# A graph layer pair: the first pair's X and W2 loaded in halves, its hop 2 taken by chunks

## The chip, the cores and the metric
The kernel runs on one core of one Trainium2 chip. The metric is the device time of one execution in microseconds. A profiled execution gives, beside its time, a span: from the first to the last instruction that the profiler recorded.

## The reference
64 graphs of 128 nodes with 256 features, an adjacency `adj` per graph. Two layers, each followed by a residual sum and a layer norm:

```python
def _L0_gnn_ref(X, A, Wv, bv, aw, ab, Wk, bk):
    Xw = X @ Wv + bv
    sj = Xw @ aw[:d, 0]
    si = Xw @ aw[d:, 0]
    e = leaky_relu(sj[:, None, :] + si[:, :, None] + ab[0], 0.2)
    alpha_matrix = A * exp(e)
    transition = alpha_matrix / (sum(alpha_matrix, -1, keepdims=True) + 1e-12)
    H = 0; Xk = X
    for k in range(3):
        H = H + Xk @ Wk[k] + bk[k]
        Xk = einsum('bij,bjd->bid', transition, Xk)
    return relu(H)
def _L1_gnn_ref(x, adj, w):
    return einsum('bnf,fo->bno', einsum('bnm,bmf->bnf', adj, x), w)
x = _layernorm(x + _L0_gnn_ref(x, adj, ...))
x = _layernorm(x + _L1_gnn_ref(x, adj, L1_gnn_w))
```

## The kernel before
The 64 graphs are worked on as 32 pairs. X comes transposed (`xt`), 128 features per partition row and two chunks `c` of the contraction over 256 features; in SBUF a pair's X is laid out chunk, graph, node, so the first 256 columns are chunk 0 of both graphs. W2 (`Wk[2]`) lies in `WY_sb` with the two chunks of its rows beside each other.

The hops are reordered: a pair's products are X W2 ("hop 2", to `ps_y`), then the transition times that plus X W1 ("hop 1", `ps_v`), then the transition times that plus X W0 ("hop 0", `ps_h`). From the second pair on each f32 product is three float32r products, of high and low parts that ScalarE (high), VectorE and GpSimd (low) split off. The first pair cannot wait for the split: `first_hop2`, `first_hop1` multiply the f32 tiles themselves; each such product shows as two matmul records.

The scores need `u`, which `score_weights` (L1177) makes from WvT and the `vectors` (aw and bv), two columns per chunk, into `ps_out`. VectorE copies u beside W1 and W2 (L575, L576), splits W2 with its u columns (L579, L581), then W0's low part (L583), and then makes the `shift` of the scores (L588). ScalarE's `first_scores` (L401) waits for hop 1 and for the shift. TensorE transposes the scores (`spread_scores`, L1084), from which ScalarE makes leaky, exp and the high part of alpha, and so on.

Each engine has its program in an order written out by hand. Five queues matter. SyncE issues the loads of X, WvT, W1; waits until X is there; then W0, X of pair 1, and so on. ScalarE issues W2, the vectors, bk, ab, and then its first activation, `XT_hi` of pair 0 (behind a load of the activation table). TensorE's order at the start is nine products of ones (`keep_warm`, 512 columns each, results unused), `first_hop2(0)` (graph 0, both chunks), `score_weights`, `first_hop2(1)`, `first_hop1(0)`, `score_shift`, `first_hop1(1)`, `sum_of_biases`, `spread_scores(0)`, `hop0(0)`, hop 2 of pair 1. VectorE's is given above. GpSimd makes bv_aw from the vectors and then the low parts of X (L901). After the opening, a loop of steps over the pairs follows, one pair per step, with products of several pairs interleaved.

Of the kernel before, what the change touches and what calls it, by code (L numbers as in the profile page):

```python
# [10 lines left out]
P = 128  # L11
PER = 2
DMA = 16
# [5 lines left out]
def resnorm_graph_kernel(nc, xt, adjs, nodes, WvT, vectors, ab, Wk, bk, w, si_rows, out):  # L19
    PAIRS = nodes.shape[0]  # L20
    D = w.shape[0]
    C = D // P
# [3 lines left out]
    with ExitStack() as ctx:  # L26
        def sb(name, shape, dt=F32):
            return ctx.enter_context(nc.sbuf_tensor(name, shape, dt))

        def ps(name, shape):  # L30
            return ctx.enter_context(nc.psum_tensor(name, shape, F32))

        def sem(name):
            return ctx.enter_context(nc.semaphore(name))


        xt_sb = [sb(f"xt{s}", [P, C * PER * P]) for s in range(4)]
# [7 lines left out]
        WY_sb = sb("WY_sb", [P, C, D + 2])  # L45
# [66 lines left out]
        ps_v = ps("ps_v", [P, PER, 512])  # L112
        ps_y = ps("ps_y", [P, PER, 512])
# [10 lines left out]
        xt_loaded = [sem(f"xt_loaded{s}") for s in range(4)]  # L124
        adjs_loaded = [sem(f"adjs_loaded{s}") for s in range(5)]
        nodes_loaded = [sem(f"nodes_loaded{s}") for s in range(2)]
        stored = [sem(f"stored{s}") for s in range(3)]
        WvT_loaded = sem("WvT_loaded")
        vectors_loaded = sem("vectors_loaded")
        ab_loaded = sem("ab_loaded")  # L130
        bk_loaded = sem("bk_loaded")
        Wk_loaded = [sem(f"Wk{n}_loaded") for n in range(HOPS)]
# [107 lines left out]
        def loads(k, slots=2):  # L240
            return DMA * (k // slots + 1)
# [41 lines left out]
        def _(sp):  # L283
            def load_xt(k):
                if k == 4:

                    sp.wait_ge(v1_done, 1)
                if k >= 4:
                    sp.wait_ge(xt_lo_ready, k - 3)
                sp.dma_start(xt_sb[k % 4][:], xt[k]).then_inc(xt_loaded[k % 4], DMA)  # L290
# [37 lines left out]
                sp.dma_start(to[:, :, 0:D], Wk[n].rearrange("(c p) n -> p c n", p=P)).then_inc(Wk_loaded[n], DMA)  # L328


            load_xt(0)
            sp.dma_start(WvT_sb[:], WvT.rearrange("(c p) n -> p c n", p=P)).then_inc(WvT_loaded, DMA)
            load_Wk(1)
            sp.wait_ge(xt_loaded[0], DMA)
# [39 lines left out]

        @block.scalar
        def _(act):
            act.dma_start(WY_sb[:, :, 0:D], Wk[2].rearrange("(c p) n -> p c n", p=P)).then_inc(Wk_loaded[2], DMA)
            act.dma_start(vectors_sb[:].rearrange("p c n -> p (c n)"), vectors).then_inc(vectors_loaded, DMA)
            act.dma_start(bk_sb[:], bk).then_inc(bk_loaded, DMA)
            act.dma_start(ab_col[:], ab.partition_broadcast(P)).then_inc(ab_loaded, DMA)  # L380

            def xt_hi(k):

                act.wait_ge(xt_loaded[k % 4], loads(k, 4))
                act.activation(XT_hi[k % 7][:].rearrange("p c b i -> p (c b i)"),  # L385
                               xt_sb[k % 4][:], ACT.Copy).then_inc(xt_hi_ready, 1)
# [108 lines left out]
            def step(k):  # L495
# [23 lines left out]
                if there(k + 6):  # L519
                    xt_hi(k + 6)  # L520
# [11 lines left out]
                if k == LAST - 1:  # L532
                    late_sum_of(LAST - 3)

            xt_hi(0)
            wx_hi(0)
            v2_hi(0)
            xt_hi(1)
            first_scores()
            xt_hi(2)  # L540
# [30 lines left out]
        def _(dve):  # L571
# [3 lines left out]
            dve.tensor_copy(W1_sb[:, :, D:D + 2], ps_u).then_inc(u_ready, 1)  # L575
            dve.tensor_copy(WY_sb[:, :, D:D + 2], ps_u).then_inc(u_ready, 1)  # L576
            dve.wait_ge(u_ready, 2)
            dve.wait_ge(Wk_loaded[2], DMA)
            dve.tensor_copy(WY_hi[:], WY_sb[:]).then_inc(WY_hi_ready, 1)  # L579
            dve.wait_ge(WY_hi_ready, 1)  # L580
# [419 lines left out]
        def _(pe):  # L1000
# [25 lines left out]
            def first_product(to, weights, b):  # L1026

                X = xt_sb[0][:].rearrange("p (c b i) -> p c b i", c=C, b=PER)
                for c in range(C):
                    last = pe.matmul(to, X[:, c, b], weights[:, c], start=c == 0, stop=c == C - 1,  # L1030
                                     skip_group_check=True)
                return last

            def first_hop2(b):
                pe.wait_ge(xt_loaded[0], DMA)
                pe.wait_ge(Wk_loaded[2], DMA)
                last = first_product(ps_y[:, b, 0:D], WY_sb[:, :, 0:D], b)
                if b == PER - 1:
                    last.then_inc(y_done, 1)

            def first_hop1(b):

                pe.wait_ge(Wk_loaded[1], DMA)
                pe.wait_ge(u_ready, 1)
                last = first_product(ps_v[:, b, 0:D + 2], W1_sb, b)
                if b == PER - 1:
                    last.then_inc(v1_done, 1)
# [99 lines left out]
            def keep_warm(to, times):  # L1147

                for n in range(times):
                    pe.matmul(to, some[:, 0:P], some, start=True, stop=True, skip_group_check=True)  # L1150
# [26 lines left out]
            def score_weights():  # L1177

                pe.wait_ge(vectors_loaded, DMA)
                pe.wait_ge(WvT_loaded, DMA)  # L1180
                for c in range(C):
                    for j in range(C):
                        last = pe.matmul(ps_u[:, c], WvT_sb[:, j, c * P:(c + 1) * P], vectors_sb[:, j, 0:2],
                                         start=j == 0, stop=j == C - 1, skip_group_check=True)
                last.then_inc(u_done, 1)
# [38 lines left out]
                    aggregate(k - 1)  # L1224
                hop2_and_scores(k + 5, [1] if k == 1 else range(PER))

            keep_warm(ps_v[:, 0], 9)
            first_hop2(0)
            score_weights()
            first_hop2(1)  # L1230
            first_hop1(0)
            score_shift()
            first_hop1(1)
# [64 lines left out]
```

## Time and profile before

| | us |
|---|---|
| median of 3 runs (277.46 to 281.25) | 277.48 |
| profiled execution, its time | 277.04 |
| profiled execution, its span | 275.2 |
| TensorE busy | 268.7 (98%) |
| VectorE busy | 210.8 (77%) |
| GpSimd busy | 196.8 (72%) |
| ScalarE busy | 188.8 (69%) |

Busy times are sums over instructions in the profiled execution; an engine busy for 98% of the span still may hold short waits. PE is TensorE, PEld its weight load, DVE VectorE, ACT ScalarE, POOL GpSimd, SP SyncE; SPq and ACTq are their queues, which issue DMAs. The median is 0.44 us above the profiled execution's time.

### The profile page before, as it was taken

Reading aid. Unit: us, or ns where it says so; the run is one execution under the profiler, and the core shown is the slowest. Engines: PE = TensorE matmul, PEld = TensorE weight load, DVE = VectorE, ACT = ScalarE, POOL = GpSimd, SP = SyncE. Lnnn points to the kernel's source line nnn. Section 1 sums busy time; section 2 is a strip of 40 time slices with the busy share of each in tenths; the row PEclk is TensorE's granted clock in tenths of the full one; section 3 lists DMA queues with packets and bytes.
Section 4 is the critical chain, followed back from the end, with each engine's and each line's share of the span. In section 5 each row is a group of like instructions: output and inputs, shape, how many; then the busy total and the mean of one; then the engine's idle time right before and its main releaser. Section 6 shows DMA issues by size and latency. Waiting matters only on the chain.

```text
span 275.2 us, 6489 instructions
## 1 busy us (share of the span) xinstructions
PE 268.7 (98%) x2199; PEld 263.0 (96%) x2199; DVE 210.8 (77%) x562; ACT 188.8 (69%) x428; POOL 196.8 (72%) x420
## 2 busy tenths in 40 slices
PE   8999999999999999999999999999999999999992
PEld 4899999999999999999999999999999999999991
DVE  0787887877778787777878777787877777788874
ACT  2788866677766677776667777666777765666643
POOL 3565577778877777887777788777777777557574
PEclk9999999999999999999999999999999999999998
DMA  7955367957845585348585278556773394912304
GB/s 228 301 138 79 117 101 172 116 132 111 148 128 157 154 144 70 126 138 153 141 154 151 81 110 137 147 148 155 133 97 51 108 124 105 126 50 80 114 0 152
DMA packets 28614, 34.92 MB, mean 127 GB/s; under 512 B 7075, under 2 KB 16422, under 8 KB 28582
## 3 DMA queue, kind: packets, MB, share of 16 engines
q1 hardware_dynamic: 27872, 33.99, 58.1%
q10 hardware_dynamic: 710, 0.53, 0.6%
q8 instruction: 17, 0.28, 0.4%
q14 instruction: 15, 0.12, 0.1%
HBM read 26.09 MB, written 8.42 MB: 125 GB/s over the span
## 4 chain that ended last, share of the span: by engine, by line
PE 91%; DVE 3%; POOL 2%; DMA 1%; issue 1%; ACT 0%; DVEq 0%; POOLq 0%
PE ps_h L1004 24%; PE ps_v L1004 17%; PE ps_y L1004 15%; PE ps_out L1004 14%; PE ps_agg L1160 10%; PE ps_v L1100 3%; PE ps_v L1104 3%; PE ps_v L1102 3%; DMA WY_sb<-Wk_dram 1%; PE ps_agg L1004 1%; PE ps_y L1030 1%; PE ps_v L1030 1%; POOL rstd L877 1%; POOL res L888 0%; DVE WX_lo L817 0%
## 5 line engine op out<-in xcount | busy, mean ns | idle before, releaser
L642 DVE SCALAR_TENSOR_TENSOR ps_h<-ps_h,inv_rowsum,bias 128x256 f32<-128x256 f32 x60 | 26.5, 488 | 22.7 <-PE ps_h L1004 22.7
L901 POOL TENSOR_TENSOR XT_lo<-xt,XT_hi 128x512 fp32r<-128x512 f32 x32 | 41.5, 1300 | 3.0 <-ACT XT_hi L385 1.4
L913 POOL TENSOR_TENSOR alpha<-exps,adjs 128x256 f32<-128x256 f32 x31 | 22.9, 738 | 23.3 <-ACT exps L428 23.3
L1004 PE MATMUL ps_v<-WX_hi,XT_hi 128*128 128x256 f32 x128 | 36.7, 287 | 0.3 <-DVE ps_v L648 0.2
L1004 PE MATMUL ps_v<-WX_lo,XT_hi 128*128 128x256 f32 x128 | 36.0, 282 | 0.0
L1004 PE MATMUL ps_v<-WX_hi,XT_lo 128*128 128x256 f32 x128 | 36.0, 281 | 0.0
L1004 PE MATMUL ps_h<-WX_hi,XT_hi 128*128 128x256 f32 x124 | 35.0, 282 | 0.0
L1004 PE MATMUL ps_h<-WX_lo,XT_hi 128*128 128x256 f32 x124 | 35.0, 282 | 0.0
L1004 PE MATMUL ps_h<-WX_hi,XT_lo 128*128 128x256 f32 x124 | 34.9, 282 | 0.0
L459 ACT ACTIVATE y<-res,offset,rstd 128x256 f32<-128x256 f32 x62 | 33.6, 591 | 1.6 <-POOL offset L868 1.5
L917 POOL TENSOR_TENSOR alpha_lo<-alpha,alpha_hi 128x256 fp32r<-128x256 f32 x31 | 22.7, 733 | 15.9 <-ACT alpha_hi L437 15.9
L1004 PE MATMUL ps_y<-WY_hi,XT_hi 128*128 128x258 f32 x112 | 34.1, 304 | 0.0
L1160 PE MATMUL ps_agg<-adjs,y 128*128 128x128 f32 x248 | 32.7, 274 | 0.0
L1004 PE MATMUL ps_y<-WY_lo,XT_hi 128*128 128x258 f32 x112 | 31.7, 283 | 0.0
L1004 PE MATMUL ps_y<-WY_hi,XT_lo 128*128 128x258 f32 x112 | 31.7, 283 | 0.0
L1004 PE MATMUL ps_out<-w_hi,agg_hi 128*128 128x256 f32 x112 | 31.6, 282 | 0.0
L1004 PE MATMUL ps_out<-w_hi,agg_lo 128*128 128x256 f32 x112 | 31.3, 279 | 0.0
L1004 PE MATMUL ps_out<-w_lo,agg_hi 128*128 128x256 f32 x112 | 31.3, 279 | 0.0
L443 ACT ACTIVATE ps_v<-ps_v,inv_rowsum 128x256 f32<-128x256 f32 x62 | 25.2, 444 | 8.5 <-DVE inv_rowsum L636 8.5
L452 ACT ACTIVATE V_hi<-ps_v 128x512 fp32r<-128x512 f32 x32 | 19.1, 595 | 17.4 <-PE ps_v L1004 17.3
L1160 PEld LDWEIGHTS ps_agg<-adjs,y 128*128 128x128 f32 x248 | 30.2, 191 | 0.0
L895 POOL TENSOR_SCALAR out_sb<-res,rstd,offset 128x256 f32<-128x256 f32 x54 | 29.5, 557 | 0.1
(165 smaller groups left out, 915.5 us busy)
## 6 DMA issues: line engine op xcount, KB each, us to landing
xt<-xt_dram SPq DMA_DIRECT2D x32, 256.0 KB, 5.2
nodes<-nodes_dram SPq DMA_DIRECT2D x32, 256.0 KB, 5.7
out_dram<-out_sb SPq DMA_DIRECT2D x30, 256.0 KB, 5.0
adjs<-adjs_dram SPq DMA_DIRECT2D x32, 128.0 KB, 5.5
spread<-si_rows_dram SPq DMA_DIRECT2D x29, 128.0 KB, 4.7
W_sb<-Wk_dram SPq DMA_DIRECT2D x2, 256.0 KB, 3.8
si_rows_dram<-scores SPq DMA_DIRECT2D x29, 1.0 KB, 4.0
WY_sb<-Wk_dram ACTq DMA_DIRECT2D x1, 256.0 KB, 3.8
```

Source lines behind the costliest of these rows:

```text
L443: last = act.activation(ps_v[:, b, 0:D], ps_v[:, b, 0:D], ACT.Copy, scale=inv_rowsum[k % 2][:, b:b + 1])
L452: act.activation(V1_hi[:], ps_v[:, :, 0:D], ACT.Copy).then_inc(v1_hi_ready, 1)
L459: last = act.activation(y[k % 3][:, b], res1[:, b], ACT.Identity, bias=offset1[:, b:b + 1], scale=rstd1[:, b:b + 1])
L642: last = dve.scalar_tensor_tensor(ps_h[:, b], ps_h[:, b], inv_rowsum[k % 2][:, b:b + 1], bias[:], ALU.mult, ALU.add)
L895: last = pool.tensor_scalar(out_sb[k % 3][:, b], res2[k % 2][:, b], rstd2[k % 3][:, b:b + 1], offset2[k % 3][:, b:b + 1], ALU.mult, ALU.add)
L901: pool.tensor_tensor(XT_lo[k % 7][:].rearrange("p c b i -> p (c b i)"), xt_sb[k % 4][:], XT_hi[k % 7][:].rearrange("p c b i -> p (c b i)") ...
L913: pool.tensor_tensor(alpha[:], exps[:], adjs_sb[k % 5][:], ALU.mult).then_inc(alpha_ready, 1)
L917: pool.tensor_tensor(alpha_lo[k % 2][:], alpha[:], alpha_hi[k % 2][:].bitcast(F32), ALU.subtract).then_inc(alpha_lo_ready, 1)
L1004: last = pe.matmul(to, a, b, start=start and n == 0, stop=stop and n == 2, skip_group_check=True)
L1100: pe.matmul(ps_v[:, b, 0:D + 2], alpha_hi[k % 2][:, b], V2_hi[k % 4][:, b], start=True, stop=False, skip_group_check=True)
L1102: pe.matmul(ps_v[:, b, 0:D], alpha_hi[k % 2][:, b], V2_lo[k % 4][:, b], start=False, stop=False, skip_group_check=True)
L1160: last = pe.matmul(agg(k)[:, c, b], y[k % 3][:, b, c * P:(c + 1) * P], adjs_sb[k % 5][:, b], start=True, stop=True, skip_group_check=True)
```

## The change
X of pair 0 is loaded by two DMAs on SyncE, one for each chunk, with a semaphore each; W2 by two on ScalarE, likewise. `first_hop2` takes a chunk and a graph and issues one product, waiting for the semaphores of that chunk's halves alone. TensorE's order becomes eight products of ones, chunk 0 of graph 0, chunk 0 of graph 1, chunk 1 of graph 0, `score_weights`, chunk 1 of graph 1. ScalarE's `xt_hi(0)` and VectorE's split of W2 wait for both halves.

```diff
-            load_xt(0)
+            sp.dma_start(xt_sb[0][:, 0:PER * P], xt[0, :, 0:PER * P]).then_inc(first_xt_chunk_loaded, DMA)
+            sp.dma_start(xt_sb[0][:, PER * P:C * PER * P], xt[0, :, PER * P:C * PER * P]).then_inc(xt_loaded[0], DMA)
             sp.dma_start(WvT_sb[:], WvT.rearrange("(c p) n -> p c n", p=P)).then_inc(WvT_loaded, DMA)
             load_Wk(1)
             sp.wait_ge(xt_loaded[0], DMA)
...
-            act.dma_start(WY_sb[:, :, 0:D], Wk[2].rearrange("(c p) n -> p c n", p=P)).then_inc(Wk_loaded[2], DMA)
+            act.dma_start(WY_sb[:, 0, 0:D], Wk[2, 0:P]).then_inc(first_WY_chunk_loaded, DMA)
+            act.dma_start(WY_sb[:, 1, 0:D], Wk[2, P:C * P]).then_inc(Wk_loaded[2], DMA)
...
             def xt_hi(k):
+                if k == 0:
+                    act.wait_ge(first_xt_chunk_loaded, DMA)
                 act.wait_ge(xt_loaded[k % 4], loads(k, 4))
...
             dve.wait_ge(u_ready, 2)
+            dve.wait_ge(first_WY_chunk_loaded, DMA)
             dve.wait_ge(Wk_loaded[2], DMA)
...
-            def first_hop2(b):
-                pe.wait_ge(xt_loaded[0], DMA)
-                pe.wait_ge(Wk_loaded[2], DMA)
-                last = first_product(ps_y[:, b, 0:D], WY_sb[:, :, 0:D], b)
-                if b == PER - 1:
+            def first_hop2(c, b):
+
+                pe.wait_ge(xt_loaded[0] if c else first_xt_chunk_loaded, DMA)
+                pe.wait_ge(Wk_loaded[2] if c else first_WY_chunk_loaded, DMA)
+                X = xt_sb[0][:].rearrange("p (c b i) -> p c b i", c=C, b=PER)
+                last = pe.matmul(ps_y[:, b, 0:D], X[:, c, b], WY_sb[:, c, 0:D], start=c == 0, stop=c == C - 1,
+                                 skip_group_check=True)
+                if c == C - 1 and b == PER - 1:
                     last.then_inc(y_done, 1)
...
-            keep_warm(ps_v[:, 0], 9)
-            first_hop2(0)
+            keep_warm(ps_v[:, 0], 8)
+            first_hop2(0, 0)
+            first_hop2(0, 1)
+            first_hop2(1, 0)
             score_weights()
-            first_hop2(1)
+            first_hop2(1, 1)
             first_hop1(0)
```

## Rows read from the trace of the kernel before

**Rows 1.** The page: busy time, share of the span, instructions.

```profile
PE 268.7 (98%) x2199; PEld 263.0 (96%) x2199; DVE 210.8 (77%) x562; ACT 188.8 (69%) x428; POOL 196.8 (72%) x420
```

**Rows 2.** Stretches: start:end, sum, busy us (instructions) per engine, granted clock, DMA share, GB/s.

```profile
0.00:4.00 4.00, 3.25 (x8) 1.17 (x9) 0.17 (x1) 1.28 (x1) 1.00 (x13) 1.00 0.46 143
4.00:10.00 6.00, 5.74 (x30) 4.28 (x28) 3.18 (x7) 2.81 (x7) 3.01 (x5) 1.00 0.99 300
...
60.00:100.00 40.00, 40.00 (x340) 40.00 (x340) 31.54 (x84) 28.50 (x65) 31.00 (x65) 1.00 0.64 125
```

**Rows 3.** Chain of waits from its beginning: start us, us, what.

```profile
0.73 3.79 DMA WY_sb<-Wk_dram
```

**Rows 4.** Timeline, TensorE, 4.5 to 7.5 us: start, us, line, operation [idle before].

```profile
4.65 1.10 PE L1030 MATMUL ps_y<-WY_sb,xt 128*128 128x256 f32 x4 [0.27 <-DMA WY_sb<-Wk_dram]
5.59 1.00 PE L1183 MATMUL ps_out<-vectors_sb,WvT_sb 128*128 128x2 f32 x8
6.45 1.11 PE L1030 MATMUL ps_y<-WY_sb,xt 128*128 128x256 f32 x4
7.40 0.38 PE L1030 MATMUL ps_v<-W_sb,xt 128*128 128x258 f32 x1
```

**Rows 5.** Line 1150, the products of ones: ns min/median/max, first and last start.

```profile
L1150 PE MATMUL ps_v<-const-bfloat16-1.0 x9: 381/631/631, 0.8 to 4.0; 128*128 128x512 bf16 x9
```

**Rows 6.** Timeline, TensorE, 3.95 to 4.05 us: eighth and ninth product of ones.

```profile
3.69 0.69 PE L1150 MATMUL ps_v<-const-bfloat16-1.0 128*128 128x512 bf16 x2
```

**Rows 7.** DMA issues before 2.5 us: count, KB, us from issue to landing.

```profile
xt<-xt_dram SPq DMA_DIRECT2D x1, 256.0 KB, 3.1
...
WvT_sb<-WvT_dram SPq DMA_DIRECT2D x1, 256.0 KB, 4.1
W_sb<-Wk_dram SPq DMA_DIRECT2D x1, 256.0 KB, 4.5
vectors_sb<-vectors_dram ACTq DMA_DIRECT2D x1, 3.0 KB, 4.3
```

**Rows 8.** Timeline, 0.7 to 1.7 us, the issuing queues of SyncE and ScalarE.

```profile
0.72 0.38 SPq L290 DMA_DIRECT2D xt<-xt_dram  x1
0.73 0.47 ACTq L377 DMA_DIRECT2D WY_sb<-Wk_dram  x1
...
1.16 0.42 SPq L332 DMA_DIRECT2D WvT_sb<-WvT_dram  x1
...
1.23 0.48 ACTq L378 DMA_DIRECT2D vectors_sb<-vectors_dram  x1
...
1.63 0.46 SPq L328 DMA_DIRECT2D W_sb<-Wk_dram  x1
```

**Rows 9.** DMA queues, 3.0 to 4.0 us, ScalarE's: packets, MB, share.

```profile
q10 hardware_dynamic: 268, 0.26, 73.8%
```

**Rows 10.** Stretches, with the columns of rows 2.

```profile
2.25:2.50 0.25, 0.25 (x2) 0.09 (x1) 0.00 (x0) 0.00 (x0) 0.00 (x0) 1.00 0.07 8
```

**Rows 11.** Timeline, VectorE, 6 to 9.3 us.

```profile
6.63 0.16 DVE L575 COPY W_sb<-ps_out 128x4 f32<-128x4 f32 x1 [5.67 <-PE ps_out L1183]
...
6.90 0.92 DVE L579 CAST WY_hi<-WY_sb 128x516 fp32r<-128x516 f32 x1
...
8.47 0.69 DVE L583 TENSOR_TENSOR WX_lo<-W_sb,WX_hi 128x512 fp32r<-128x512 f32 x1
9.07 0.21 DVE L588 TENSOR_SCALAR shift<-ps_agg,ab_col 128x1 f32<-128x1 f32 x1
```

**Rows 12.** Timeline, ScalarE, 2 to 10 us.

```profile
2.72 1.28 ACT L385 ACT_TABLE_LOAD   x1 [2.72 <-issue]
...
9.57 0.26 ACT L401 ACTIVATE scores<-ps_v,shift 128x4 f32<-128x4 f32 x1 [0.85 <-PE ps_v L1030]
```

**Rows 13.** Timeline, TensorE, the first transposes of the scores.

```profile
10.09 0.43 PE L1084 MATMUL ps_out<-identity,scores 128*128 128x128 f32 x2
```

**Rows 14.** Timeline, GpSimd, 5 to 8 us.

```profile
6.27 1.27 POOL L901 TENSOR_TENSOR XT_lo<-xt,XT_hi 128x512 fp32r<-128x512 f32 x1
```

More of the change, by code:

```diff
@@ L127, in resnorm_graph_kernel @@
         stored = [sem(f"stored{s}") for s in range(3)]
+        first_xt_chunk_loaded = sem("first_xt_chunk_loaded")
+        first_WY_chunk_loaded = sem("first_WY_chunk_loaded")
         WvT_loaded = sem("WvT_loaded")
```

## The prediction

> **What bounds the kernel now.** I read the stretches first. From 60 to 100 us TensorE is busy in 40.00 of 40.00 us, and over the whole span in 98%; between 4 and 10 us it lacks a quarter of a microsecond [rows 1, 2]. In the steady part nothing can be taken off but TensorE's own work, which the change leaves alone. What the opening saves or loses therefore moves the end by the same amount, as long as TensorE stays the engine that is late; and what the opening can save is small against 275.2 us.
>
> The chain of waits then says what starts TensorE's real work: the load of W2, issued at 0.73, landed 3.79 us later, at 4.52 [rows 3]. The first product of X with W2 starts at 4.65, so landing to product is 0.13 us. Behind it TensorE's order runs without a hole: two products in four records at 4.65, the eight records of score_weights at 5.59, two more products at 6.45, hop 1 at 7.40 [rows 4]. So four records of 256 columns take 0.94 us at the opening of a run and 0.95 later, 0.22 each with 0.07 for the first; the eight small ones take 0.86.
>
> **The eight products of ones.** The nine start at 0.76, the eighth at 3.69 and the last at 4.0; their median is 631 ns, and one lasts 381 [rows 5, 6]. The granted clock reads 1.00 [rows 2], these microseconds included, yet 512 columns pass in 0.42 us (3.69 minus 0.76, over seven), which is the lower level, 1.2 GHz. From the eighth to the ninth it is 0.31: the rise fell into the eighth, and the ninth's 381 ns and the 0.22 us of the f32 records belong to 2.4 GHz. With one product fewer TensorE is free at 4.0 (where the ninth began), at the latest at 4.1 (eight times 0.42 behind 0.76). The product removed is worth nothing while the loads end later than that.
>
> **The halves, step by step.** X lands 3.1 us after its issue at 0.72, at 3.8; WvT 4.1 after 1.16, at 5.26; the vectors 4.3 after 1.23, at 5.53; W1 4.5 after 1.63, at 6.13 [rows 7, 8]. From X to W2 to WvT it is 0.7 us each, which is 256 KB at some 370 GB/s: the loads come in the order of their issue and wait for bytes, not for the queue that issues them. All of W2's 256 packets, with 12 small ones, pass between 3.0 and 4.0 [rows 9], and the semaphore follows some 0.55 us behind. Half of W2 should then be through at about 3.5 and land at 4.07, with all of X ahead of it: X's second half, issued some 0.4 later than the first, has its bytes in the same place as before. Then the first product can start at 4.07 + 0.13 = 4.20, 0.45 earlier than now, and the ones' end does not hold it. Bounds for this half: not before 3.8 (X itself is 128 packets and landed then), not after 4.52. I take 4.07, because the packets stand in time order.
>
> The Trainium skill, page "DMA: Bandwidth & Descriptors", section "Anatomy of one DMA", fits a DMA as 2.0 us plus bytes over 436 GB/s (for the GpSimd path). By that, as an estimate, half of the bytes land only 0.30 us earlier, at 4.22, and the first product would start at 4.35; no row of before shows a half.
>
> **What comes behind it.** After the change three products (six records, 0.94 + 0.43 = 1.37 us) stand before score_weights instead of two. From 4.20 they end at 5.57, and score_weights waits for the vectors, which land at 5.53: it starts at 5.59, as now. The last product then takes 0.45 instead of 0.95, and hop 1 starts at about 6.96 instead of 7.40. W1 is there at 6.13, the copy of u at 6.79 [rows 11]. So TensorE gains 0.44 up to here, and all of it comes from a product done while the vectors were still on their way.
>
> But VectorE's chain hangs on score_weights, which has not moved: copies of u at 6.63, WY_hi 6.90, WY_lo behind it, WX_lo 8.47, and only then, in VectorE's order, the shift at 9.07, which ends at 9.28 [rows 11]. The first scores on ScalarE wait for hop 1 and for the shift. Today hop 1 is the late one: the scores start at 9.57, released by TensorE [rows 12]. With hop 1 done at 9.53 - 0.44 = 9.09 the shift is late next, and the scores start at about 9.31: 0.26 earlier, not 0.44. The transposes of the scores (now 10.09) follow them, and hop0, hop 2 of pair 1 and the whole alpha chain follow those [rows 13]. Expected of the order alone: -0.26 us.
>
> **The queues.** ScalarE's queue issues one more load, 0.47 us; SyncE's one more, 0.38 to 0.42 [rows 8]. ScalarE: vectors, bk and ab go out 0.47 later; the table load (2.72, 1.28 long) and XT_hi of pair 0 slip by as much, XT_hi's end to about 5.1 [rows 12]. Nobody minds that: GpSimd's XT_lo starts at 6.27, behind the sums of bv_aw, which by the code wait for the vectors [rows 14]. SyncE: WvT and W1 go out about 0.4 later, and W0 waits for X's second half instead of the whole, about the same moment. What it costs depends on whether the landing follows the issue or the bytes. If the bytes, nothing; if the issue, the vectors land at 6.00 and all behind score_weights is 0.47 late. A gain is excluded, since they sit behind the same bytes. Between 0 and 0.47 I take 0.1, near the lower end: the vectors land 4.3 us after their issue and X 3.1 after its own, so some 1.2 us of theirs is queueing and 0.47 fits into that, but there are now two more DMAs ahead.
>
> **Sum.** -0.26 + 0.1 = about -0.16. The extra wait in ScalarE, VectorE and TensorE on the new semaphores is for things landed long before the next one: 0, hidden by the wait behind it. The profiled run took 277.04 us, so 276.9 by its measure; the median of the runs is 277.48, 0.44 above it, and set against that the sum gives 277.3. This spread is larger than the effect.
>
> **Rivals.**
> **A, the halves do not come earlier.** If the halves share the transfer's packets so that the first lands with the whole, at 4.52, the product starts at 4.65 as now, with three products before score_weights: it starts at 6.03, 0.44 late. VectorE's chain goes with it, the shift ends at 9.72, scores at 9.75 instead of 9.57: 0.18 us slower, 277.65. In general the result is -0.26 plus the first product's delay behind 4.20; it turns slower once the first half of W2 lands after 4.33. For it: the stream starts haltingly, with 8 GB/s between 2.25 and 2.5 us, while X is on its way, which no byte count explains [rows 10]; halves may add to that. Against it: packets stand in order. Chance 0.22. The Trainium skill's page "DMA: Bandwidth & Descriptors", section "Rules for kernel authors", tells against this change: of two transfers to disjoint partition halves it says "Don't bother", since they serialize over the same engines. These halves are of columns, and by that rule the time is this rival's.
> **B, the loads behind slip.** The vectors land 0.47 late (ScalarE's issue) up to 0.88 (both queues' extra issues added). Then score_weights and the shift are late by that: -0.26 + 0.47 = +0.21, up to +0.62, 277.7 to 278.1. It decides from 0.26 us of slip on. For it: the vectors landed 1.0 us behind W2, with only WvT's bytes (0.7) between. Against it: the landings of the large loads are spaced by bytes. Chance 0.15.
> **C, the shift is no cover.** If VectorE runs the shift earlier than I read, the full 0.44 stays: 277.0. Its order is fixed in the code, so 0.08.
> **D, the clock.** With eight products of ones, the rise to 2.4 GHz may come after TensorE's first real products. Each 256-column record then costs 0.21 more; if it lasts until 7.40, eight records make 1.7 and the eight small ones up to 0.8: 279.5. Against it: in this trace the rise fell into the eighth product, before the ninth, and the real work follows the eighth without a hole. Chance 0.07.
> My forecast, a gain of 0 to 0.3 us, has the remaining 0.48.
>
> **Range and chances.** A to C lie between 277.0 and 278.1; with the scatter between the profiled run and the median I take 276.8 to 278.1, which leaves D and the ends of the noise outside. A gain or loss over 2% (5.5 us, about what can be told from no change here) has no case: 0.01 each, 0.98 within.
>
> **What would show it.** The chain should begin with the first half of W2, landing near 4.07, and the first product of X and W2 near 4.2. In TensorE's order six records, then score_weights at 5.59 (later means A or B; which, the landing of the vectors tells), hop 1 near 6.96. The first scores should start 0.26 before 9.57 and be released by VectorE's shift; a release by TensorE speaks for A or C. The records behind the eighth product of ones must be 0.22 apart, or D holds. If the scores come 0.26 earlier and the end doesn't, the passing-on of a shift through the steady part is what I have wrong.

## The result, and the profile after

The changed kernel took 278.34 us (median of 22 runs, 277.03 to 280.11), the kernel before beside it 277.53 (22 runs): a ratio of 1.0036, interval 1.0018 to 1.0053. Within 2% that is no change, but the interval leaves out 1: the medians differ by 0.8 us, the ratio is worth 1.0, where 277.3 and a range up to 278.1 were forecast. Ratios here and below leave out executions marked as slow (lower granted clock, or over 1.5% above the fastest of their kernel). The profiled execution took 279.52 us with a span of 277.0, 1.8 more than before's span; it is 1.2 above its own median, so its profile shows one of the costly executions and not the usual one.

First the loads of the opening, against [rows 7]: DMA issues of the changed kernel before 2.5 us (count, KB, median us from issue to landing).

```profile
xt<-xt_dram SPq DMA_DIRECT2D x2, 128.0 KB, 2.8
WY_sb<-Wk_dram ACTq DMA_DIRECT2D x2, 128.0 KB, 3.0
WvT_sb<-WvT_dram SPq DMA_DIRECT2D x1, 256.0 KB, 3.9
W_sb<-Wk_dram SPq DMA_DIRECT2D x1, 256.0 KB, 4.2
vectors_sb<-vectors_dram ACTq DMA_DIRECT2D x1, 3.0 KB, 3.7
```

Taken one at a time, the first halves landed 2.6 (X) and 2.8 us (W2) behind issues at 0.72 and 0.73, at 3.3 and 3.5; the second half of W2 3.2 behind 1.17, at 4.4; the vectors 3.7 behind 1.65, at 5.35. These are earlier than I had said. The rest is not: X's second half took 3.0 behind 1.16 and landed at 4.2, where the whole of X had landed at 3.8; WvT landed at 5.5 (before 5.26), W1 at 6.3 (6.13).

TensorE's timeline of the changed kernel from 3.3 us on, against [rows 4, 13] (start, us, line, operation):

```profile
4.12 2.53 PE L1047 MATMUL ps_y<-WY_sb,xt 128*128 128x256 f32 x6
6.50 0.95 PE L1194 MATMUL ps_out<-vectors_sb,WvT_sb 128*128 128x2 f32 x8
7.30 0.68 PE L1047 MATMUL ps_y<-WY_sb,xt 128*128 128x256 f32 x2
...
10.55 0.43 PE L1095 MATMUL ps_out<-identity,scores 128*128 128x128 f32 x2
```

The six records start at 4.12, directly behind the eighth product of ones, but take 2.53 us instead of 1.37: the first five are 0.43 apart, the lower level of the clock, although the granted clock of this stretch reads 1.00, as in [rows 2]. So score_weights starts at 6.50 instead of 5.59, 0.91 late. Half of that comes back, because one product stands behind it instead of two: hop 1 starts at 7.82 instead of 7.40, and since the scores are still released by hop 1, the transposes come at 10.55 instead of 10.09. The opening costs 0.46 us.

The stretches say that this is not all. From 20 to 60 us (columns of [rows 2]; the kernel before has 39.93 us of TensorE in the same stretch):

```profile
20.00:60.00 40.00, 38.87 (x323) 38.29 (x322) 30.67 (x82) 28.82 (x70) 27.00 (x54) 1.00 0.69 118
60.00:100.00 40.00, 40.00 (x340) 40.00 (x340) 31.76 (x85) 28.31 (x66) 30.81 (x65) 1.00 0.65 130
```

TensorE's timeline has one wait there:

```profile
40.64 0.39 PE L1012 MATMUL ps_h<-V_hi,alpha_hi 128*128 128x256 f32 x1 [1.07 <-DVE V_lo L661]
```

The chain of waits of the changed kernel leads back from it (start, us, what):

```profile
28.43 2.15 SPq L318
...
30.63 0.43 SPq L305
...
31.10 0.89 DMA adjs<-adjs_dram
...
34.94 0.43 ACT exps L435
35.37 2.83 issue
38.19 0.75 POOL alpha L921
...
38.96 0.42 ACT alpha_hi L444
39.38 0.49 ACT V_hi L459
...
39.90 0.70 DVE V_lo L661
...
40.64 0.98 PE ps_h L1012 x6
...
43.74 1.31 PE ps_h L1012 x11
```

The same places in the kernel before: SyncE's queue from 27 to 29 us, and GpSimd's alpha of that pair.

```profile
27.46 0.43 SPq L315 DMA_DIRECT2D si_rows_dram<-scores  x1
27.94 0.43 SPq L302 DMA_DIRECT2D nodes<-nodes_dram  x1
28.41 0.43 SPq L296 DMA_DIRECT2D adjs<-adjs_dram  x1
...
34.98 0.74 POOL L913 TENSOR_TENSOR alpha<-exps,adjs 128x256 f32<-128x256 f32 x1 [2.20 <-ACT exps L428]
```

And its chain, at the products that show the shift:

```profile
41.96 1.44 PE ps_h L1004 x12
```

SyncE's issue of the store of scores starts 0.97 late (the issue ahead of it waits for the landing of an earlier store of scores) and takes 2.15 us instead of 0.43. The two loads behind it go out late, the adjacencies of pair 4 at 31.10 instead of 28.41; they land 7.0 us later (before: 5.9), at 38.1 instead of 34.3. So the 3.8 us of lateness are 0.97 from ahead of the long issue, 1.7 from its length and 1.1 from a slower landing. GpSimd's alpha needs them at 35.4 (before at 34.9, so there were 0.6 us to spare), waits, and TensorE is idle for 1.07 us. What stands beside the long issue is one packet of instructions: the DMA queues of the changed kernel from 27.5 to 28.0 us have nothing else,

```profile
q14 instruction: 1, 0.01, 31.3%
```

which is one of 16 engines for 2.5 us (0.313 of 16 times 0.5 us). The kernel before has such a packet of 8 KB only behind 30 us, and it takes 0.3 us (0.039 by the same sum, over 30.5 to 31.0, among other transfers):

```profile
q14 instruction: 1, 0.01, 3.9%
```

From there the offset stays: the twelve products of `ps_h` that start at 41.96 before start at 43.74 after, 1.8 late, and the span ends 1.8 late. Of this 0.46 is from the opening and some 1.3 from the late adjacencies.

A long issue is nothing new in itself. The kernel before has one of 1.81 us at 35.03, beside a packet of instructions of 16 KB on another queue (q8) that took 1.6 us, and nobody waits for what it delays. Over the twenty profiles of this case SyncE has 144 issues of over 1 us behind 20 us, of some 170 in each, and every one overlaps a packet of instructions of over 0.87 us. What is new with the change is where the first of them falls.

### The profile page after: what moved, and what is told of

It is laid out like the page before. It is cut to its first block, busy times and chain, and to the rows that moved or that the text cites. A ratio compares the mean times of both kernels' runs of the same rounds, so it can differ in the third digit from the quotient of the medians.

```text
span 277.0 us, 6492 instructions
## 1 busy us (share of the span) xinstructions
PE 269.7 (97%) x2198; PEld 263.9 (95%) x2198; DVE 210.2 (76%) x562; ACT 188.3 (68%) x428; POOL 196.6 (71%) x420
## 2 busy tenths in 40 slices
DMA packets 28774, 34.92 MB, mean 126 GB/s; under 512 B 7107, under 2 KB 16710, under 8 KB 28742
## 4 chain that ended last, share of the span: by engine, by line
PE 86%; DMA 4%; POOL 2%; ACT 2%; DVE 2%; issue 2%; SPq 1%; DVEq 0%; POOLq 0%
PE ps_h L1012 22%; PE ps_v L1012 15%; PE ps_y L1012 14%; PE ps_out L1012 13%; PE ps_agg L1171 9%; DMA si_rows_dram<-scores 3%; PE ps_v L1111 3%; PE ps_v L1115 3%; PE ps_v L1113 2%; PE ps_v L1161 1%; PE ps_y L1047 1%; SPq L318 1%; PE ps_v L1038 1%; PE ps_agg L1012 1%; POOL rstd L885 1%
## 5 line engine op out<-in xcount | busy, mean ns | idle before, releaser
L1012 PE MATMUL ps_h<-WX_hi,XT_lo 128*128 128x256 f32 x124 | 34.9, 282 | 0.0
```

The lines of the kernel that those rows point to most:

```text
L1012: last = pe.matmul(to, a, b, start=start and n == 0, stop=stop and n == 2, skip_group_check=True)
```

## The experiments

Two explanations stood at first: the clock, as in rival D of the prediction, and SyncE's long issue, set off by something that the change does to a queue or to a program. The theories' letters in the quoted expectations are explained where they stand and hold for that group alone. No kernel leaves out a part of the computation. Ratios are to the kernel before on the same chip. The first long issue is SyncE's first from 20 us on that is over 1 us, in the one profile of each.

| kernel | median us (runs) | of these over 279 us | ratio [interval] | first long issue, us |
|---|---|---|---|---|
| before | 277.53 (22) | 1 | | 1.81 at 35.03 |
| changed | 278.34 (22) | 8 | 1.0036 [1.0018, 1.0053] | 2.15 at 28.43 |
| e1_halves_nine_ones | 279.33 (6) | 5 | 1.0052 [1.0033, 1.0071] | 2.23 at 28.34 |
| e2_before_eight_ones | 277.57 (12) | 0 | 0.9994 [0.9980, 1.0007] | 1.07 at 34.62 |
| e3_halves_old_order | 278.32 (12) | 3 | 1.0005 [0.9980, 1.0031] | 2.42 at 28.33 |
| e4_whole_new_order | 277.92 (12) | 1 | 1.0003 [0.9983, 1.0023] | 1.54 at 33.90 |
| e5_x_halves | 277.93 (12) | 0 | 0.9997 [0.9980, 1.0014] | 1.51 at 35.33 |
| e6_w2_halves | 278.69 (12) | 5 | 1.0047 [1.0015, 1.0079] | 1.30 at 48.90 |
| e7_one_more_dma | 277.71 (12) | 0 | 0.9982 [0.9963, 1.0001] | 1.52 at 35.76 |
| e8_w2_halves_new_order | 278.33 (12) | 1 | 1.0003 [0.9986, 1.0020] | 1.54 at 35.26 |
| e9_two_waits_scalar | 278.88 (11) | 5 | 1.0037 [1.0019, 1.0056] | 2.10 at 28.92 |
| e10_bk_on_sync | 277.83 (12) | 0 | 1.0002 [0.9988, 1.0017] | 2.15 at 34.47 |
| e11_adjs4_early | 277.94 (12) | 0 | 1.0005 [0.9990, 1.0019] | 1.59 at 27.83 |
| e12_before_adjs4_early | 277.62 (12) | 0 | 0.9994 [0.9979, 1.0009] | 2.07 at 35.11 |
| e13_both_repairs | 277.75 (12) | 0 | 0.9998 [0.9981, 1.0015] | 1.11 at 35.96 |
| e14_longer_scalar | 278.39 (12) | 4 | 1.0028 [1.0001, 1.0054] | 2.17 at 35.05 |
| e15_changed_again | 278.64 (12) | 5 | 1.0028 [0.9997, 1.0060] | 2.04 at 28.56 |
| e16_w2_halves_again | 278.09 (8) | 1 | 1.0003 [0.9985, 1.0021] | 1.21 at 34.99 |
| e17_w2_halves_again2 | 277.67 (8) | 0 | 0.9996 [0.9980, 1.0012] | 2.05 at 34.59 |
| e18_changed_third | 277.63 (8) | 0 | 0.9990 [0.9969, 1.0010] | 1.43 at 28.59 |

Of all 170 executions of the kernel before, beside these and the changed one, 7 took over 279 us.

### The parts of the change

The changed kernel with nine products of ones (e1); the kernel before with eight (e2); the changed kernel with nine and the old order, waiting for all halves first (e3); the kernel before with whole loads and the new order (e4).

```diff
e1:
-            keep_warm(ps_v[:, 0], 8)
+            keep_warm(ps_v[:, 0], 9)
e3, in the changed kernel, beside the nine:
+            for chunk in (first_xt_chunk_loaded, first_WY_chunk_loaded, xt_loaded[0], Wk_loaded[2]):
+                pe.wait_ge(chunk, DMA)
             first_hop2(0, 0)
-            first_hop2(0, 1)
             first_hop2(1, 0)
             score_weights()
+            first_hop2(0, 1)
             first_hop2(1, 1)
```

> The changed kernel with nine products of ones instead of eight; all else as changed. Theory 1 (the clock: without the ninth, f32 products run before the rise to 2.4 GHz, at 0.43 us a record instead of 0.22, and score_weights starts at 6.50 instead of 5.59): the records of X and W2 are 0.22 apart, start near 4.4, score_weights starts at 5.6 to 5.8, and the median lies 0.5 to 1.0 us under the changed kernel's 278.34. Theory 2 (the two additional DMAs disturb the loads behind them): no gain over the changed kernel, 278.0 to 278.6. Theory 3 (the rise falls by chance, in any kernel): the records may show either spacing, and the median is near the changed kernel's.

> The kernel before with eight products of ones instead of nine. Theory 1: TensorE idles from about 4.1 to 4.65, the rise is late, the first four f32 records are 0.43 apart, and the median is 0.5 to 1.0 above the 277.5 of before. Theories 2 and 3: the same as before within 0.2 us.

> The kernel before with its loads of X and W2 in halves, TensorE waiting for all four before its first product, the old order of products, nine products of ones: the DMAs alone. Theory 1: as before, 277.5 within 0.3. Theory 2: slower by 0.5 to 1.0, 278.0 to 278.5.

> The kernel before with the changed order of products alone (three of hop 2 ahead of score_weights), whole loads, nine products of ones. By the prediction's sum the first product stays at 4.65, score_weights slips by 0.44 to 6.03 and the first scores by 0.18: 277.7. Theories 1 and 2 both say this; if it is 278.3 the order alone is the cause.

With the ninth product back the loss stays (e1), and without it the kernel before loses nothing (e2): the count of ones is not the cause. The new order alone is worth nothing (e4); there score_weights starts at 6.04, which is where rival A of the prediction had it. The long issue near 28 us is in the two kernels with all four halves and in neither of the others. The clock falls as the main cause.

e3's ratio shows no loss, though it has the long issue. Its profile is of an execution of 282.05 us, one of two over 282, and shows what the same wait can cost: the adjacencies landed 8.5 us behind their issue, TensorE was idle for 2.77 us, and a microsecond after it had begun again its granted clock fell to the lower level until 46.3 (columns of [rows 2]):

```profile
43.10:46.30 3.20, 3.20 (x17) 3.20 (x16) 1.80 (x5) 2.84 (x7) 3.04 (x7) 0.50 0.85 98
```

By the exps of the table further down, this execution lost 4.6 us across the wait, 2.8 of them idle.

### Which half, and is it one more DMA?

X alone in halves (e5) and W2 alone in halves (e6), both in the old order behind waits for all of them; the kernel before with one more small load on SyncE (e7); W2 alone in halves in the new order (e8).

```diff
e7:
             load_xt(0)
+            sp.dma_start(spare[:], ab.partition_broadcast(P)).then_inc(spare_loaded, DMA)
             sp.dma_start(WvT_sb[:], ...).then_inc(WvT_loaded, DMA)
```

> Only X of pair 0 loaded in halves (one more DMA on SyncE's queue), W2 whole, TensorE waiting for both halves of X and for W2, nine products of ones, the old order of products. Theory Q (one more DMA on SyncE's queue moves a stall of that queue, 1.07 to 1.81 us and at 34 to 35 us where the loads are whole, to 28.4 us with 2.15 to 2.42 us where they are in halves; there the load of an adjacency slips, and TensorE loses 1.1 to 2.8 us between 38 and 42): the stall is at 28.4, TensorE loses over 0.5 us between 20 and 60, and the median is 0.5 to 1.5 above the kernel before. Theory K (the late rise of the clock alone is the loss): TensorE is full from 20 to 60 us and the median is as before.

> Only W2 loaded in halves (one more DMA on ScalarE's queue), X whole, TensorE waiting for both halves of W2 and for X, nine products of ones, the old order. Theory Q: SyncE's queue is as before, no stall over 2 us at 28.4, TensorE full from 20 to 60, median within 0.3 of the kernel before. If the bytes or packets of the opening are the cause and not SyncE's queue: as in the previous one, 0.5 to 1.5 above.

> The kernel before with one more DMA on SyncE's queue behind X's: 512 bytes (ab broadcast to a spare column), awaited only at the end. Nothing else is changed, no load is halved. Theory Q: the stall moves to about 28.4 us, TensorE loses 0.5 to 2.8 us between 20 and 60, the median is 0.5 to 1.5 above the kernel before. If it is the halving and not the number: as before within 0.3.

> The changed kernel with X whole and nine products of ones: W2 in halves and the new order of products. Theory Q: SyncE's queue is as before, so the steady part is whole; the opening gains what the halves of W2 give when the clock has risen by 4.2 us (scores 0.2 to 0.3 earlier) and loses up to 0.5 when it rises at 6: the median within -0.3 and +0.3 of the kernel before. If it is 1 us slower, the new order or W2's halves carry the loss and Theory Q falls.

None has a long issue near 28 us, so one more DMA on either queue does not make it. e6 is slower all the same, by another way: in its profile the second half of W2 landed at 4.96, the first product started at 5.17 and the transposes at 11.12, 1.0 late. Its ratio also rests on two groups of executions: seven from 277.8 to 278.9, one of 279.99, and four of 281.3 to 281.5, of which no profile was taken. e8 has the same halves and no loss in its ratio. What then do e1, e3 and the changed kernel have alone? In the compiled programs ScalarE's is two instructions longer than before (567 against 565: one more DMA, one more wait); in e5, e6 and e8 it is one longer, in e2, e4 and e7 none. (These counts are read from the compiled programs; no trace shows them.)

### ScalarE's program alone

e9 is the kernel before with three waits on ScalarE that are long fulfilled, no DMA, no other order: its compiled program becomes two instructions longer, 567 as well. e10 is the changed kernel with the load of bk moved to SyncE, so that ScalarE's program is one shorter (566). e14 is the kernel before with eight more (573), by pairs of fulfilled waits at eight places of its start.

```diff
e9, before ScalarE's xt_hi(0):
+            act.wait_ge(ones_ready, 1)
+            act.wait_ge(pool_setup, 4)
+            act.wait_ge(identity_ready, 1)
             xt_hi(0)
e10, SyncE and ScalarE of the changed kernel:
             load_Wk(1)
+            sp.dma_start(bk_sb[:], bk).then_inc(bk_loaded, DMA)
...
-            act.dma_start(bk_sb[:], bk).then_inc(bk_loaded, DMA)
```

> The kernel before with ScalarE's program two instructions longer (567 as in the changed kernel, instead of 565) by waits for what is long done: ones, GpSimd's constants and the identity. No DMA is added, no load halved, no order changed. Theory L (the stall of SyncE's queue at 28.4 us comes from where the fetch of instructions falls: it was there in all three kernels whose ScalarE program has 567 instructions, and in none of the seven with 565 or 566, two DMAs more or less): a stall over 2 us at 28.4, an instruction packet of some 2.5 us at 27.5 to 28.3, TensorE loses 0.5 to 2.8 us between 20 and 60, median 0.5 to 1.5 over the kernel before. Theory N (it comes from two more DMAs in all): as before within 0.3, no such stall.

> The changed kernel with the load of bk issued by SyncE behind W1 instead of by ScalarE: as many DMAs, ScalarE's program 566 instructions. Theory L: no stall over 2 us at 28.4, TensorE full from 20 to 60, median 0.5 to 1.2 us under the changed kernel, within 0.3 of the kernel before. Theory N: as the changed kernel.

> The kernel before with ScalarE's program eight instructions longer (573) by waits on things long done, in its opening. Theory L as a threshold (from 567 on the fetch comes early): a stall near 28.4 or earlier, median 0.5 to 1.5 over the kernel before. If 567 was a coincidence of position, the stall moves off again and the median is within 0.3 of the kernel before.

e9 and e10 are the experiments that decide. In e9 nothing but ScalarE's program has changed, and it is slower by 0.37%, where the changed kernel is by 0.36%. Five of its 11 executions took over 279 us; of the 34 of the kernel before on the same chip none did, nor any of the 12 of e10. The queue of SyncE in e9, and GpSimd's timeline:

```profile
28.92 2.10 SPq L315 DMA_DIRECT2D si_rows_dram<-scores  x1
```

```profile
38.03 0.73 POOL L916 TENSOR_TENSOR alpha<-exps,adjs 128x256 f32<-128x256 f32 x1 [4.60 <-issue]
```

and the only packet that starts in its DMA queues from 28 to 29 us, again in the silence, one engine for 2.6 us:

```profile
q14 instruction: 1, 0.01, 16.3%
```

Not all of e9's profile is this. W2 landed at 4.97 there (before 4.52), much as in the profiles of e6 and e12, and its transposes came 0.62 late. The exps of pair 4 and those of two pairs on (34.49 and 50.55 in the kernel before) show how much was lost ahead of the adjacencies' wait and how much across it:

| profile | exps of pair 4 | two pairs on | late by, then | late by, now |
|---|---|---|---|---|
| changed | 34.94 | 52.36 | 0.45 | 1.81 |
| e1 | 35.06 | 52.39 | 0.57 | 1.84 |
| e3 | 34.92 | 55.56 | 0.43 | 5.01 |
| e9 | 35.14 | 52.19 | 0.65 | 1.64 |
| e15 | 35.39 | 52.64 | 0.90 | 2.09 |
| e18 | 35.45 | 51.55 | 0.96 | 1.00 |
| e10 | 34.70 | 50.77 | 0.21 | 0.22 |

The wait costs 1.0 to 1.4 us in the changed kernel, e1, e9 and e15, 4.6 in e3, and nothing in e18.

e9's waits also hold back ScalarE's own start: its table load begins at 4.34, behind the landing of X, instead of 2.72. That alone is not the cause, since e10's begins at 4.22 and the changed kernel's at 4.21.

e10 has all the halves and the new order, no long issue near 28 us, and no loss: the store of scores takes 0.43 us as before, and TensorE is busy throughout.

```profile
27.61 0.43 SPq L318 DMA_DIRECT2D si_rows_dram<-scores  x1
```

```profile
20.00:60.00 40.00, 40.00 (x334) 39.64 (x333) 31.96 (x83) 30.31 (x72) 28.02 (x55) 1.00 0.60 121
```

e10 does have an issue of 2.15 us, as long as the changed kernel's, but at 34.47, where TensorE waits for nothing behind it.

In every profile without a long issue near 28 us, no packet of this queue stands between 27 and 30 us (they come behind 30; e14 has one at 26 to 27, of 0.3 us); in every profile with one, a packet stands there with 1.5 to 2.8 us of its engine. The first packet of the queue behind 20 us moves with ScalarE's program in all twenty profiles: it starts between 30.9 and 32.5 with 565 or 566 instructions, between 27.6 and 28.5 with 567, and at 26.1 with 573. e14 shows that it is the place and not the length that counts: eight instructions more move the packet to before 27 us, and TensorE has 39.93 of 40 us as before. Its ratio of 1.0028, whose interval just leaves out 1, and its four executions over 279 us are not explained by this; its one profile is of 278.05.

### The slack of pair 4's adjacencies

The same load moved into the opening, in the changed kernel (e11) and in the kernel before (e12); e13 is e10 with this, and VectorE's `v1_lo(0)` ahead of `WX_lo[1]`.

```diff
                     load_nodes(1)
+                    load_adjs(4)
                 if there(k + 1) and k > 0:
                     load_nodes(k + 1)
-                if there(k + 3) and k > 0:
+                if there(k + 3) and k > 1:
                     load_adjs(k + 3)
```

> The changed kernel with the load of pair 4's adjacency issued in the opening, behind the nodes of pair 1, instead of behind the stalled store of scores. ScalarE's program is unchanged at 567. If the adjacency of pair 4 is what the stall delays (alpha of pair 4 started 2.8 us behind its exponentials, and TensorE idled 1.1 us): the stall stays at 28.4, TensorE's loss between 20 and 60 falls to under 0.3 us, and the median is 0.5 to 1.2 under the changed kernel. If the scores' own round trip is the path, nothing changes.

> The kernel before with the load of pair 4's adjacency issued in the opening. In the profile of before it landed 0.6 us ahead of its need, so little is to be had: the median within 0.2 of before, its slow runs (over 1 us above the lowest) fewer if they come from this load.

> The changed kernel with bk loaded by SyncE (ScalarE's program 566 instructions), the adjacency of pair 4 loaded in the opening, and VectorE making V1's low part of pair 0 ahead of W1's low part. Theory G (with bk on SyncE the opening was 0.39 us ahead at the transposes and nothing was left of it at 19.4, because GpSimd's alpha of pair 1 and VectorE's W1 low part, 1.30 and 0.68 us, now ran into each other and GpSimd's XT_lo of pair 4 ended as late as before): with them apart alpha takes 0.74, hop 2 of pair 4 starts near 19.1 where the clock rises early, and the median is 0.1 to 0.3 under the kernel before. Otherwise: within 0.2 of it.

e11 still has the issue of 1.59 us (now the load of nodes, at 27.83), but nobody waits for it: TensorE is busy in 40.00 of 40 us from 20 to 60, the ratio is 1.0005, and none of its 12 executions took over 279 us (e9, on the same chip, has five of 11). So the loss goes by way of the adjacencies. The executions say so more than the profile, since an issue of only 1.43 us cost nothing in e18 with the load in its old place. The move itself is worth nothing (e12). e13, meant to beat both kernels, does not: GpSimd's alpha took 0.74 again, as Theory G wanted, but in its profile the first six records took 2.52 us and the transposes came at 10.54.

### More profiles of the same programs

> The changed kernel as it is, once more, for a second profile. Theory L: again a stall over 2 us of SyncE's queue near 28 and TensorE short by 0.5 us or more between 20 and 60. Theory of chance for the clock: the f32 records may be 0.22 or 0.43 apart, whatever the first profile of it showed. Median 0.5 to 1.2 over the kernel before.

> The same program as the kernel with W2 in halves, whole X and the new order, once more for another profile; nothing is left out of the computation. Its spans so far were of two kinds, about 275.4 and about 276.5 us, and its one profile was of the first kind (275.6), without a stall. Theory S (the stall of SyncE's issue makes the longer ones too): if this profile's span is 276.2 or more, one of SyncE's issues between 27 and 30 us takes over 1.5 us, and an instruction packet of queue 14 stands there with a share above 10% of its microsecond; if it is 275.8 or less, neither is there and the two packets come behind 30 us. Rival O (the opening makes them): in a span of 276.2 or more the first transposes of the scores start at 10.7 or later (0.6 late), and there is no issue over 1 us at that place.

> The same program a third time, for the same question: Theory S wants a span of 276.2 or more only together with an issue of SyncE over 1.5 us between 27 and 30 us; Rival O wants it with transposes of the scores at 10.7 or later and no such issue. Seven of twelve spans so far were 276.4 or more, so one of these two profiles should be a long one.

> The changed kernel a third time. Its spans so far ran from 275.7 to 277.3. Theory S: if the span is 276.4 or more, the stall of over 1.5 us is there between 27 and 30 us; a span of 275.9 or less has no stall, or one that ends early enough for pair 4's adjacencies (issue of their load before 29.5). Rival O: the spread comes from the clock in the opening: a short span has its first six records in 1.3 to 1.6 us, a long one in 2.0 to 2.5 us, with the stall in both.

e15 repeats the profile after: the long issue, alpha 4.8 us idle, a span of 277.3, though its six records took 1.60 us and not 2.53. In e18, the same program, the long issue was shorter (1.43) and fell one DMA later: the adjacencies went out at 30.06 and landed 6.2 later, alpha waited till 36.36, TensorE for nothing between 38 and 40. Its median does not differ from before. Its span of 276.2 is the opening's and the stretch up to 20 us. So the changed kernel pays in some executions and not in others: 8 of 22, 5 of 12 and none of 8 took over 279 us, and over these sets the ratio was 1.0036, 1.0028 and 0.9990. The first and the last interval do not meet, so one set's interval says less than it seems to, for e9 and e10 too, of which there is one set each.

e16 and e17 were for the spans of about 276.5 in a kernel without the long issue. e16 caught one (276.6), e17 a short one (275.6), and Rival O of that expectation is right. e16's VectorE and GpSimd at 9 us, then e17's:

```profile
9.09 1.75 DVE L588 TENSOR_TENSOR WX_lo<-W_sb,WX_hi 128x512 fp32r<-128x512 f32 x1
10.76 0.20 DVE L593 TENSOR_SCALAR shift<-ps_agg,ab_col 128x1 f32<-128x1 f32 x1
```

```profile
8.98 1.31 POOL L906 TENSOR_TENSOR XT_lo<-xt,XT_hi 128x512 fp32r<-128x512 f32 x1 [0.82 <-ACT XT_hi L389]
```

```profile
9.03 0.69 DVE L588 TENSOR_TENSOR WX_lo<-W_sb,WX_hi 128x512 fp32r<-128x512 f32 x1
```

```profile
9.09 1.75 POOL L906 TENSOR_TENSOR XT_lo<-xt,XT_hi 128x512 fp32r<-128x512 f32 x1 [0.99 <-ACT XT_hi L389]
```

In e16 GpSimd starts 0.11 us ahead and VectorE's instruction takes 1.75 us; in e17 VectorE starts 0.06 ahead and GpSimd's does. Only in the first does anyone wait: the shift comes at 10.76, and the transposes at 11.43 behind an idle 1.05 us of TensorE, against 10.43 in e17. The Trainium skill, page "SBUF — State Buffer", section "Who interferes with whom", says that a VectorE instruction with two inputs in SBUF contends with a GpSimd instruction that reads SBUF, and that issue order decides who blocks; these rows agree, with 1.06 us for the one that comes second.

## Why the prediction was wrong

**The step that failed** is "Nobody minds that", said of ScalarE's program with one more load and one more wait. In the sum it stands again as "0" for the extra wait. I priced the queue and the slip of ScalarE's own work. The slip was three times what I gave (the table load at 4.21, behind the landing of X's second half, where 3.2 was meant; XT_hi's end at 6.14, where I said 5.1), but nobody waited for it in the changed kernel. What I left out is that with the longer program a packet of instructions stands at 27 to 29 us instead of behind 30, beside it an issue of SyncE takes 2.15 us, and the adjacencies of pair 4 had 0.6 us to spare. e9 shows this path without the change, 1.0 us across the wait; e10 shows the change without it. That the packet belongs to ScalarE and that its slow transfer holds up SyncE's issue is inferred: it follows ScalarE's program, both last about as long, and every long issue of every profile has such a packet beside it. Which of the two holds up the other no run shows.

The Trainium skill, page "Runtime: NRT & Kernel Launch", section "Instruction fetch mechanics", calls the cost of crossing a block of instructions "mostly hidden". For the fetching engine no run here shows otherwise; but the DMA issue of another engine took 2.10 us beside such a packet in e9.

**"What the opening saves or loses therefore moves the end by the same amount"** held for losses in most profiles: e16's 1.3 us, and the changed kernel's 0.46 up to 35 us. e7 is an exception, 0.8 late at 10 and at 50 us and 0.1 at its last stores; why was not looked into. It did not hold for a gain. e10 had the predicted opening, its scores released by the shift:

```profile
9.34 0.27 ACT L408 ACTIVATE scores<-ps_v,shift 128x4 f32<-128x4 f32 x1 [0.79 <-DVE shift L596]
```

I had said 9.31, and "the shift is late next" was right; the transposes came at 9.70, 0.39 earlier. But 6 us on, GpSimd's alpha met VectorE's `WX_lo` of the next weight and took 1.30 us; before it was 0.74, and VectorE's took 1.05:

```profile
15.58 1.30 POOL L921 TENSOR_TENSOR alpha<-exps,adjs 128x256 f32<-128x256 f32 x1 [1.32 <-ACT exps L435]
...
18.10 1.30 POOL L909 TENSOR_TENSOR XT_lo<-xt,XT_hi 128x512 fp32r<-128x512 f32 x1
```

TensorE's next product waited for that low part until 19.45, where the same product starts at 19.24 before. This is what the prediction named as its last sign of being wrong: the scores earlier, the end not. The gain was gone, and the twelve records of `ps_h` began at 26.71 against 26.50. Between 10 and 20 us GpSimd, not TensorE, is the late engine; I had read the stretch from 4 to 10 and the one from 60 to 100, and nothing between.

**The halves.** That the first halves land earlier was right, and rivals A and B were false in this profile: the first half of W2 landed at 3.5 (I said 4.07) and the vectors at 5.35 (5.53 to 5.63), a gain that I had excluded. So the end of the ones, at 4.12, held the first product, and not the load. The worth is small all the same, since the chain goes by score_weights, which waits for the vectors and for WvT. X's second half and WvT landed 0.3 to 0.4 later than I had taken them: in e15 score_weights waited 0.29 us for WvT, till 6.02, which is rival B by another load.

**The clock** (rival D, 0.07) did occur in the profile after, at a smaller price than I gave: 0.46 us at the transposes instead of 2. The new order gave half of the 0.91 back. VectorE did not stand in the way either: its copy of W2 took 0.43 us there instead of 0.92, as GpSimd's XT_lo (6.22 to 7.5) was done by then. When the clock rises differs between executions: the six records took 2.53, 1.60, 2.30 us in three profiles of the changed kernel and 1.56 in e10, and in e7, with whole loads and nine products of ones, four records took 2.01 instead of 1.10. A first product at 4.12 instead of 4.65 can put more records ahead of the rise; how much of the 0.46 is that, no run separates.

**Scatter.** The profiled execution before (277.04) lay below the median, as I had said; its slack of 0.6 us at pair 4 was never looked up. Two sums were off, without bearing on the result: 5.59, 0.86 and 0.45 give hop 1 at 6.90 and not 6.96, and rival D's terms on 277.3 give 279.8 and not 279.5.

What stays open: why a packet at this place is slow (in silent DMA engines) and at others takes 0.3 us; whether it delays the issue or the issue it; how often it costs in the changed kernel; whether another edit of ScalarE's program to the same length does the same; and the ratios of e6 and e14.

## What to carry to other kernels

An edit that adds instructions to an engine's program can move the packets of instructions behind it (here one of them from 30.9 to 28 us). When a change of "no cost" loses a few tenths of a per cent, compare the issues of SyncE far behind the edit, and build the kernel before with as many fulfilled waits as a control. Take several sets of runs of each: one program gave 1.0036 and 0.9990 here. Before pricing a gain in the opening, look in every later stretch for the engine that is late, and for pairs of VectorE and GpSimd instructions that start within a few tenths of a microsecond of each other. Loads with under a microsecond of slack are where such noise turns into time.

## What the runs showed of the hardware

- A packet of instructions of 8 KB took 0.3 us of its DMA engine in the kernel before and 2.5 in the changed one, with no other transfer beside it; the DMA issue next to it took 2.15 us instead of 0.43. All 144 issues of SyncE over 1 us in twenty profiles overlap a packet of instructions of over 0.87 us.
- The products' spacing showed 1.2 GHz (0.43 us for each f32 record of 256 columns) in stretches whose granted clock reads 1.00, and how long it did so differed between executions of one program: 1.60 to 2.53 us for six records.
- The first halves of 128 KB landed 2.6 (X) and 2.8 us (W2) behind their issue, the second 3.0 and 3.2, the whole 256 KB 3.1 and 3.79. In other profiles the whole took 2.8 to 3.5 and 3.5 to 4.2.
- In e3 TensorE was idle for 2.77 us, worked for 0.8 at a granted clock of 1.00, and then had 0.50 for 3.2 us. Behind the changed kernel's idle 1.07 us it stayed at 1.00.
- Which of VectorE and GpSimd starts first, by 0.1 us, decided 1.0 us of span (e16, e17).
